# Wide attention: the subtraction of the maxima done four side by side, two maxima steps in every key block, and double bf16 copies of q and k

## The reference

```
Q = (x @ Wq.T + bq).reshape(B, N, H, HD)
K = (x @ Wk.T + bk).reshape(B, N, H, HD)
V = (x @ Wv.T + bv).reshape(B, N, H, HD)
scores = jnp.einsum('bnhd,bmhd->bhnm', Q, K)
scores = scores * (SCALE * adaptive_scale)[None, :, None, None] / TEMP
w = jax.nn.softmax(scores, axis=-1)
attn = jnp.einsum('bhnm,bmhd->bnhd', w, V).reshape(B, N, H * HD)
y = x + (attn @ Wo.T + bo)
```

## Time and profile before

| | |
|---|---|
| median of 3 runs | 6034.11 us |
| the profiled execution: its time, its span | 6037.21 us, 6035.4 us |
| busy in the whole span: TensorE, VectorE, ScalarE, GpSimd | 5572.8, 3966.0, 2749.3, 1091.7 us |
| the stage's first and last score | 3999.8 us, 5479.7 us |

### The profile page before, as it was taken

How to read it: one execution, slowest core, us unless ns; L and a number is a source line. 1 busy time by engine, 2 the same in 40 slices (tenths; PEclk the granted TensorE clock), 3 DMA queues, 4 the chain that set the end, 5 groups by cost and what they waited for, 6 DMA issues and landing times. The chain is left out here.

```text
span 6035.4 us, 88534 instructions
## 1 busy us (share of the span) xinstructions
PE 5572.8 (92%) x33238; PEld 2852.0 (47%) x33238; DVE 3966.0 (66%) x6791; ACT 2749.3 (46%) x4388; POOL 1091.7 (18%) x731
## 2 busy tenths in 40 slices
PE   7999998788989999989999899979999999997999
PEld 2333333345467777742222377733343433434776
DVE  6777775774577777769999523267777777773412
ACT  4656565222233333337777633334444344342333
POOL 0110100130022222311220000023434333331000
PEclk7999999788989999989999899989999999998999
DMA  4211110001211111111111100000000000001000
GB/s 86 45 30 29 30 29 11 0 0 27 38 28 25 32 26 30 28 17 35 35 35 27 35 1 1 1 23 12 15 8 15 12 12 12 12 15 36 4 4 8
DMA packets 119148, 131.42 MB, mean 22 GB/s; under 512 B 44580, under 2 KB 67924, under 8 KB 118404
## 3 DMA queue, kind: packets, MB, share of 16 engines
q1 hardware_dynamic: 118216, 125.07, 10.1%
q10 hardware_dynamic: 504, 0.69, 0.1%
HBM read 102.29 MB, written 22.07 MB: 21 GB/s over the span
## 5 line engine op out<-in xcount | busy, mean ns | idle before, releaser
L583 DVE TENSOR_REDUCE l_max_parts<-l_p 128x2 f32<-128x1024 f32 x512 | 602.2, 1219 | 189.6 <-PE l_p L559 153.7
L729 ACT ACTIVATE attn_w<-l_p 128x512 f32<-128x512 f32 x1024 | 554.8, 596 | 366.1 <-PE l_p L719 256.1
L3432 DVE TENSOR_REDUCE wide_max_parts<-wide_p 128x2 f32<-128x1024 f32 x512 | 613.6, 1219 | 132.9 <-PE wide_p L3336 120.5
L2389 PE MATMUL caus_p<-caus_x_one,big 128*128 128x129 f32 x4608 | 639.3, 286 | 0.0
L583 DVE TENSOR_REDUCE rot_max_parts<-rot_p 128x2 f32<-128x1024 f32 x512 | 601.4, 1218 | 50.9 <-PE rot_p L559 48.5
L2467 ACT ACTIVATE big<-caus_p 128x512 f32<-128x512 f32 (+3 forms) x768 | 345.4, 489 | 590.8 <-PE caus_p L2375 439.0
L2389 PEld LDWEIGHTS caus_p<-caus_x_one,big 128*128 128x128 f32 x4608 | 589.9, 198 | 35.8 <-issue 2.8
L2824 ACT ACTIVATE moe_hidden<-moe_experts,moe_b 128x512 f32<-128x512 f32 x512 | 351.0, 687 | 527.0 <-PE moe_experts L2812 526.9
L3355 PE MATMUL wide_p<-wide_q,wide_k 64*128 64x512 f32 x2048 | 526.6, 593 | 0.0
L3535 ACT ACTIVATE attn_w<-wide_p 128x1024 f32<-128x1024 f32 x342 | 350.1, 1024 | 348.9 <-PE wide_p L3355 345.4
L2834 PEld LDWEIGHTS moe_experts<-big,moe_hidden 128*128 128x128 f32 x4096 | 474.2, 192 | 50.3 <-issue 49.3
(11 more groups left out here) (535 smaller groups left out, 8313.0 us busy)
## 6 DMA issues: line engine op xcount, KB each, us to landing
pair_q_stack<-q_parts SPq DMA_DIRECT2D x576, 32.0 KB
pair_k_stack<-k_parts SPq DMA_DIRECT2D x576, 32.0 KB
wide_inverse<-inverse_rows SPq DMA_DIRECT2D x64, 256.0 KB
l_q_stack<-q_parts SPq DMA_DIRECT2D x279, 32.0 KB
l_k_stack<-k_parts SPq DMA_DIRECT2D x279, 32.0 KB
big<-in_L_ffn_W SPq DMA_DIRECT2D x32, 256.0 KB, 5.6
q_parts<-pair_parts_q SPq DMA_DIRECT2D x8, 768.0 KB, 3.6
k_parts<-pair_parts_k SPq DMA_DIRECT2D x8, 768.0 KB, 3.6
```

Of the source, the lines that this page charges most:

```text
L583: self.nc.vector.tensor_reduce(self.max_parts[:, 2 * p:2 * p + 2, n, half], pair[:, :, 0:self.width(n, half)], AX.X, ALU.max).then_inc(*se ...
L729: self.nc.scalar.activation(self.exps[t % len(self.exps)], bank, ACT.Exp).then_inc(*self.exped.up())
L2389: mm = nc.tensor.matmul(outs[o % 2][:, nq % 2 * (C + 1):(nq % 2 + 1) * (C + 1)], exps[h % 2][:, kb, nq * P:(nq + 1) * P], x_one[b % 2][:, ...
L3432: nc.vector.tensor_reduce(max_parts[:, :, n, h], side, AX.X, ALU.max).then_inc(*maxed.up())
```

## The change

1. The subtractions of both score steps of a key block are now issued together, ahead of both: four products with 32 rows each (`quarter`) instead of two times two with 64. Each writes one bank. For this `max_rows` has 512 columns instead of 1024, its rows 0 and 1 of each quarter of the partitions are filled by 8 transfers instead of 4, and TensorE waits for the slots of both score steps before the four.
2. The two scores of a key block stand next to each other in the list; behind them comes one other step (`later`, `sums`, one of the three projections in key blocks 3, 4 and 5, or `send` in key block 6), then one maxima step, `weigh` and `add`, then a second maxima step.
3. The maxima run on as one stream over all units, four steps further ahead than their unit's scores, so that unit u+1's maxima are complete after key block 5 of unit u (`send` moved from key block 7 to 6).
4. `q_bf` and `k_bf` are kept twice.
5. `add_beside` of a key block is tied to the second maxima step of the same key block; before, to a maxima step of the next.

```
-    MAXIMA = [3, 2, 3, 2, 2, 2, 2, 0]
...
+    stream = [("max", u, t) for u in range(1, len(units)) for t in range(TILES)]
+
+    def maxima(n):
+        out = []
+        for _ in range(min(n, len(stream))):
+            out.append(stream.pop(0))
+            out += beside(out[-1])
+        return out
+
+    plan = project(0) + [("max", 0, t) for t in range(TILES)] + [("send", 0)] + project(1) + maxima(4)
     for u in range(len(units)):
         for kb in range(NT):
+            plan += [("score", u, kb, h) for h in range(HALF)]
+            if kb == NT - 2:
+                plan += [("send", u + 1)] if u + 1 < len(units) else []
+            elif kb == 1:
+                plan += [("sums", u - 1)] if u else []
+            elif kb in (3, 4, 5):
+                plan += [project(u + 2)[kb - 3]] if u + 2 < len(units) else []
+            else:
+                plan += next_later()
+            plan += maxima(1)
             plan += beside(None)
             if kb:
                 plan += [("weigh", u, kb - 1), ("add", u, kb)]
                 waiting.append((u, kb))
             elif u:
                 plan += [("weigh", u - 1, NT - 1), ("keep", u - 1)]
+            plan += maxima(1) + gate_work(IN_TILE)
+            if u and kb == 3:
                 plan.append(("invert", u - 1))
             elif u and kb == 5:
                 plan.append(("divide", u - 1))
...
                     cols = slice(h * BANK, (h + 1) * BANK)
-                    for a in range(2):
-                        nc.tensor.matmul(side[:, a, :], ones_bf[own[a], :], max_rows[u % 2][own[a], cols],
-                                         start=True, stop=False)
+                    if h == 0:
+
+                        _, i_next, left_next = plan[n_step + 1]
+                        if left_next and new(*left_next):
+                            pe.wait_ge(*left_next[0].at(left_next[1]))
+                        for half, to in enumerate((side, slots[i_next])):
+                            for a in range(2):
+                                rows_of = quarter[HALF * a + half]
+                                nc.tensor.matmul(to[:, a, :], ones_bf[rows_of, :],
+                                                 max_rows[u % 2][rows_of, :], start=True, stop=False)
```

More of the change, by code:

```diff
@@ L3112, in wide_attention @@
     v_tok = [st.sbuf(f"v_tok{i}", [P, NT, C]) for i in range(SLOTS)]
-    q_bf, k_bf = st.sbuf("q_bf", [P, T], BF16), st.sbuf("k_bf", [P, T], BF16)
+    q_bf, k_bf = ([st.sbuf(f"{n}_bf{i}", [P, T], BF16) for i in range(2)] for n in "qk")
     ones_bf = st.sbuf("ones_bf", [P, P], BF16)
-    max_rows = [st.sbuf(f"max_rows{i}", [P, T], BF16) for i in range(2)]
+    max_rows = [st.sbuf(f"max_rows{i}", [P, BANK], BF16) for i in range(2)]
+    quarter = [slice(j * P // 4, (j + 1) * P // 4) for j in range(4)]
     E_BUFS = 6
@@ L3172, in beside @@
         return [("add_beside", *waiting.pop(0), step)] if waiting else []
-    plan = project(0) + [("max", 0, t) for t in range(TILES)] + [("send", 0)] + project(1)
+    stream = [("max", u, t) for u in range(1, len(units)) for t in range(TILES)]
[6 more added lines that the diff above has]
+    plan = project(0) + [("max", 0, t) for t in range(TILES)] + [("send", 0)] + project(1) + maxima(4)
     for u in range(len(units)):
-        todo = list(range(TILES)) if u + 1 < len(units) else []
         for kb in range(NT):
-            for h in range(HALF):
-                plan.append(("score", u, kb, h))
-                for _ in range((MAXIMA[kb] + h) // HALF if todo else 0):
-                    plan.append(("max", u + 1, todo.pop(0)))
-                    plan += beside(plan[-1])
-            plan += beside(None)
-            if kb == NT - 1 and u + 1 < len(units):
-                plan.append(("send", u + 1))
-            if u + 2 < len(units):
-                if kb == NT - 1:
-                    plan += [("project_k", u + 2), ("project_v", u + 2)]
+            plan += [("score", u, kb, h) for h in range(HALF)]
[8 more added lines that the diff above has]
+            plan += maxima(1)
+            plan += beside(None)
             if kb:
@@ L3191, in wide_attention @@
                 waiting.append((u, kb))
-                if kb == NT - 2 and u + 2 < len(units):
-                    plan.append(("project_q", u + 2))
             elif u:
                 plan += [("weigh", u - 1, NT - 1), ("keep", u - 1)]
-            plan += gate_work(IN_TILE)
-            if u and kb == 1:
-                plan.append(("sums", u - 1))
-            elif u and kb == 3:
+            plan += maxima(1) + gate_work(IN_TILE)
+            if u and kb == 3:
                 plan.append(("invert", u - 1))
@@ L3275, in _ @@
                         sp.wait_ge(*scored.at(TILES * (u - 1)))
-                    for a in range(2):
+                    n = NT // HALF
+                    for j in range(4):
                         for r, part in enumerate((max_hi, max_lo)):
-                            row = a * WIDE + r
+                            row = j * P // 4 + r
                             nc.sync.dma_start(
                                 max_rows[u % 2][row:row + 1, :].rearrange("o (n t) -> o n t", t=P),
-                                part[a * NT:(a + 1) * NT, :]).then_inc(*row_sent.up(16))
+                                part[j * n:(j + 1) * n, :]).then_inc(*row_sent.up(16))
                 elif kind == "sums":
@@ L3309, in _ @@
             pe.wait_ge(*ones_set.at(1))
-            for (kind, *args), i, left in plan:
+            for n_step, ((kind, *args), i, left) in enumerate(plan):
                 side = None if i is None else slots[i]
@@ L3346, in _ @@
                     u, kb, h = args
-                    for sem, n in ((q_kept, u + 1), (k_kept, u + 1), (row_sent, 64 * (u + 1))):
+                    for sem, n in ((q_kept, u + 1), (k_kept, u + 1), (row_sent, 128 * (u + 1))):
                         if new(sem, n):
@@ L3524, in _ @@
                                          bias=bk[:, m:m + 1]).then_inc(*k_kept.up())
-                    if u:
-                        a_.wait_ge(*max_scored.at(TILES * u))
-                    nc.scalar.activation(two(k_bf[:, :]), side, ACT.Identity,
+                    if u > 1:
+                        a_.wait_ge(*max_scored.at(TILES * (u - 1)))
+                    nc.scalar.activation(two(k_bf[u % 2][:, :]), side, ACT.Identity,
                                          bias=bk[:, m:m + 1]).then_inc(*k_cast.up())
```

14 lines of the change are left out of this document (6 added, 8 removed).

## The result

| | before | changed |
|---|---|---|
| median | 6033.47 us (4 runs, 6030.53 to 6039.41) | 6246.98 us (4 runs, 6245.55 to 6252.89) |
| ratio | | 1.0357, 95% interval 1.0343 to 1.0372 |
| profiled execution: span | 6035.4 | 6244.3 |
| mean granted clock | 0.946 | 0.947 |

The change costs 3.6%. The forecast was 6255. In the changed kernel the maxima product is L3341, the turn L3348, the projections of q and k L3324, v L3330, the subtraction L3364, the score L3367, `weigh` L3381, q's copy L3427, v's writing L3434, the reduction L3444, the joined maxima L3451, the adds L3255, the division L3467.

What follows compares the result with a forecast made beforehand. TensorE, busy 348.6 of 349 us, was taken to set the time. Terms -5 + 19 + 79 + 79 + 4 + 20 + 0 + 25 = +221 gave 6255 us beside 6034, range 6100 to 6400.

Steps and rivals of the forecast that it cites:

- key block, shapes: TensorE, 256 key blocks: one subtraction less (-0.22), two more shape changes (+0.20); -5 us, bounds -56 and +51.
- steps put between 64-row products: TensorE: projections, `send` and `sums` cost six more shape changes, 0.6 us a unit; +19 us.
- key blocks 3 and 4: TensorE waits 0.71 and 1.93 us behind q's copy and an add held by GpSimd, in 30 units; +79 us.
- key blocks 5 and 6, the turn: TensorE waits 2.65 us for joined maxima behind a held division, in 29 units, about 2 in two others; +79 us.
- rows by DMA: Eight transfers instead of four land at 18.6, next unit's first subtraction due at 18.5; +4 us, at most +30.
- gate's steps, closing steps: Gate's steps held by GpSimd in 13 units, +20 us; closing steps dealt three to a unit, 0, bounds -49 and +50.
- clock: Half clock for 3.4 us after long waits, about 1.7 us lost, in half of 30 units; +25 us (0 to 50).
- The order on TensorE: Shape changes cost 0.10 us, four 32-row products run at once; -0.02 a key block, plus +19 for steps in between.
- some 6: Sign in a steady unit's timeline: turns lie some 6 us further apart than before.
- (b): Rival: GpSimd gets in only after VectorE's add, so waits are smaller; +98, 6132 us, range 6100 to 6180, chance 0.17.
- (c): Rival: faster, free change between 32 and 64 rows, waits added under 2.9 us a unit; 5985 us, chance 0.11.
- (d): Rival: runaway in the gate's units, the add waits 2.35 us every third block; 6420 us, range 6340 to 6500, chance 0.08.

Runs made afterwards that it cites:

- experiment 1: Changed kernel with the old subtraction (64 rows, ahead of each score, four transfers instead of eight): 6268.76 us, ratio 1.0394.
- experiment 7: Kernel before with the new four-product subtraction, both scores side by side and the block's maxima steps behind them: 6142.08 us, ratio 1.0181.
- Experiment 4: Changed kernel with GpSimd's adds shrunk to 8 of 512 columns for each head: 6106.86 us, ratio 1.0122.
- experiment 8: Kernel before with a sequence's closing steps dealt one in key block 4 and two in key block 7, instead of five key blocks: 6090.76 us, ratio 1.0093.
- experiment 2: Changed kernel with q's bf16 copy moved to the end of key block 4: 6176.60 us, ratio 1.0238.
- experiment 3: Changed kernel with the division moved behind key block 6's add: 6214.71 us, ratio 1.0301.
- experiment 5: Changed kernel with q's copy moved to the end of key block 4 and the division into key block 6: 6145.58 us, ratio 1.0185.
- experiment 11: Changed kernel with the old subtraction and both q's copy and the division moved, leaving the order alone: 6135.06 us, ratio 1.0163.
- experiment 9: Kernel before with one closing step moved from key block 7 to key block 0: 6044.95 us against 6035.84, ratio 1.0018.

## Why the prediction was right, by its own steps

| step | forecast, us | measured, us |
|---|---|---|
| key block, shapes | -5 | +25 |
| steps put between 64-row products | +19 | +15, by difference |
| key blocks 3 and 4 | +79 | +76 (2.52 x 30) |
| key blocks 5 and 6, the turn | +79 | +66 (2.28 x 29) |
| rows by DMA | +4 | -2 |
| gate's steps, closing steps | +20, 0 | +7 together, by difference |
| clock | +25 | +22 |
| span | +221 | +209 |

The second line is the 47 us less the first line's 25 and the 7 that belong to the waits. The 76 and 66 are from the timeline's intervals, against the same pairs of products without a wait (0.80 and 1.72; 2.28). The waits grew by 142 us in the view by tile and by those 7, together 149; less 76 and 66 this leaves 7 for gate and closing steps. Since two lines are differences, the table closes by its making.

The sum came out within 12 us, closer than its terms. The first line was 30 too low, the others together 42 too high; that they offset each other is luck.

**The order on TensorE** is the one term with a wrong sign. The change between 32 and 64 rows costs the 0.10 that I chose, and four products do run at once. The term that was wrong is the -0.02 of a key block: missing was another 0.10 in the two scores behind the subtraction (1.82 against 2 x 0.86), 25 us over 256 blocks. Experiments 1 and 7 tie it to the 32-row products: with the old subtraction in the new order the block is 4.57, with the new one in the old order scores take 1.82. The rule of the Trainium skill on the tiling mode (TensorEngine Tiling, section Key Properties) was borne out by the steps of 0.33 and 0.32, and speaks of no cost inside the product that follows.

**Key blocks 3 and 4, 5 and 6** went step by step as written. VectorE's add behind q's copy was forecast to be done 10.15 us behind the subtraction of key block 3 and was at 10.24; the joined maxima 11.01 behind that of key block 5, and started at 11.04. The waits came out a little smaller (1.72 for 1.93, 2.28 for 2.65) because TensorE arrived 0.30 and 0.38 later, 0.20 of it through two blocks that were 0.10 longer. The turns lie 7.65 us further apart than before where some 6 was named as a sign: the missing part is the 0.10 of eight blocks and the half clock behind the turn. Experiment 4 shows the mechanism: without the shut-out 108 of the 191 us of waits are gone. The doubt whether an add is held like the division, on which rival (b) rested, is settled by the 3.00 us.

**Clock.** The size was right, the way to it less so. The eight turns from 4094.9 to 4453.9 all have a stretch of half clock behind them, where every second one was forecast; of the other 24 turns 11 have one. The larger point was missed: the clock multiplies a change of the waits. In experiment 1 blocks and waits together gave 16 us back and the clock made a loss of 22 of it, in experiment 8 it made up half of the loss.

**Gate and closing steps.** The +20 for the gate was too high, though its steps are held as forecast: L3067, on 128x8, has a median of 1.19 us instead of 0.16 (25 steps each). In the 13 turns beside them the wait is 2.58 or 2.59 instead of 2.20, which makes 5 us, and their intervals are hardly longer than those of other units, as (d) below shows. My 0 for the closing steps holds as a sum, as far as differences tell. Steps do meet GpSimd's add there: 11 of them are held in the changed kernel, 7 in the kernel before.

**The rivals.** (b) fell with the add of 3.00 us. (c) needed fewer than 2.9 us of waits in a unit and a free change of rows; there were 4.8, and it wasn't free. (d) would have shown as a wait in every third block of the gate's units. Where these have no closing steps (turns from 4780.7 to 4884.0 and from 5225.7 to 5328.6) the turns lie 51.4 to 51.7 us apart, against 51.3 in a steady unit, with only the three waits of a steady unit between them.

## What to carry to other kernels

When one engine works in order through reductions that the bound engine needs, look at what each step *beside* them reads: a VectorE add, division, copy or scaling with its operands in SBUF that starts behind a GpSimd add lasts until GpSimd's end, and up to 1.1 us more if it is a large one, however small it is by itself, and everything queued behind is late by that. Not every step that reads SBUF is held: the reciprocal kept its 0.93 each of the 5 times it started beside such an add in the kernel before. Before regrouping products to save one, count the changes of row count around them; here a saved product of 0.22 us was paid for with 0.32. And add a term for the clock to long waits: in the changed kernel none of the 30 waits of 1.65 ahead of the product for k was followed by half clock, and 19 of the 29 waits of 2.20 to 2.59 at the turn were. Then check the sum of waits, shapes and half the half-clock time against the measured difference: in experiments 1 to 5, 8 and 11 it closed within 7 us.

## What the runs showed that I had not expected

- fp32 products behind 32-row products are slower by 0.10 us for a pair of scores (1.82 for 1.72), and a small 64-row product in between doesn't take that cost over.
- A wait of 1.65 us ahead of the product for k left the clock at full every time, one of 2.56 at the same place was followed by half clock in 9 of 33 cases (3.64 us against 1.98 for the same product in the unit shown). And a wait of 2.21 at the turn was followed by 3.55 in one kernel and by 1.94 in another (experiment 2, in the unit at 4187), so its length alone doesn't decide.
- The shut-out also works backwards. In experiment 3 GpSimd's add began at 4195.93, while an add of VectorE was running (4195.02 to 4196.22), and the division right behind that add went through in its 1.21 as well; GpSimd's add took 3.65. In the changed kernel a reduction out of PSUM stood behind VectorE's add at 4192.69; there GpSimd came in after the add (3.14), and the division that followed was held (2.24). But a small step right behind a running add was held, too (4487.70 in experiment 9). What decides which of the two goes first isn't settled by these traces.
